# An attention stage reordered: maxima through four banks, rope, norm and statistics in the first part of each body, the residual on GpSimd

## The chip, the cores and the metric

The kernel runs on one core of one Trainium2 chip. The metric is the device time of one execution in microseconds (us), start to end. The engines are PE (TensorE, with its weight loads shown apart as PEld), DVE (VectorE), ACT (ScalarE), POOL (GpSimd) and SP (SyncE), which here only issues DMAs.

## The reference

Sixteen batches of 256 rows by 256 columns in float32 go through two gated layers. Layer 0 adds the normalised x times a decayed running sum of `ctx * ctx`, gated, and a feed-forward block whose inputs and hidden values are rounded to a 4-bit grid. Layer 1, which this study is about, is

```python
q = rope(norm(x)); k = rope(ctx); v = ctx            # 16 heads of 16
scores = einsum('bqhd,bkhd->bhqk', q, k) / sqrt(16) + slope[h] * (key - query)
out = einsum('bhqk,bkhd->bqhd', softmax(scores), v)
x = x + tanh(g_xattn[1]) * out
x = x + tanh(g_ffn[1]) * ffn(norm(x))                # block floating point, gelu
```

with the softmax over 256 keys of each row of each head.

## The kernel before

The whole kernel is one program written out by hand: each engine has its own list of instructions, and semaphores tie the lists together. Nothing is planned at run time, so an instruction that waits holds everything behind it on its engine. The program has three stages: layer 0 (to about 340 us of the span), attention (about 340 to 687 us) and the last feed-forward block. x (`xres`) and ctx stay in SBUF for all sixteen batches.

Attention goes batch by batch in a function `at_body(b)` on each engine. Body b works on three batches at a time:

- for batch b, PE computes the transposed scores (`at_scores`, 16 groups u of two 64-row matmuls, two banks `a_ps_s`), ACT takes the exponential (`at_exponent`), PE multiplies by the values (`at_times_v`, 8 groups), ACT copies the product out (`at_pv_out`);
- for batch b+1, PE transposes the stacked q and k (`at_turn`, 8 groups g, two banks `a_ps_t`), ACT copies them (`at_turned`), PE computes the scores once more in the other direction (`at_scores_for_max`, 16 groups m, two banks `a_ps_m`) and DVE takes the maximum of each row (`at_row_max`). PE then transposes the maxima (`at_turn_max`), ACT negates them (`at_max_out`) and SP places them by two DMAs as a row of the stack (`at_place_max`), from where they enter the scores of batch b+1 in the next body;
- for batch b+2, DVE takes the statistics (`at_qk_a`) and normalises (`at_qk_norm`), POOL multiplies by cosines and sines (`at_k_parts`, `at_q_parts`), DVE adds the halves (`at_rope`) and writes the high part (`at_high_part`), and POOL the low part (`at_low_part`): q and k enter the matmuls as two parts to keep float32 precision.

For batch b-1, PE transposes the product back (`at_turn_out`), and DVE divides by the sum of the exponentials, multiplies by the gate and adds to x (`at_add_attention`).

The order of a body on PE is: transposes 0 and 1, output of b-1, transposes 2 to 5, scores 0, transposes 6, scores 1, transposes 7 (here called the first part), then the sixteen maxima groups, each followed by a score group and, after every second score group, a value product (the second part), and at the end the turned maxima of b+1. DVE reduces in the second part, with the rope of q after five groups and its high part after eight. The two tiles `a_ps_t` and `a_ps_m` are two PSUM banks each, the four of scores and products two and two. A maxima group m waits until DVE has reduced group m-2, whose bank it takes. Bodies 14 and 15 also hold the rounding of the last block's weights (`w34_magic` on DVE, `w34_round` on POOL, `turn_w34` on PE). Body 15 has no next batch.

## Time and profile before

| what | value |
|---|---|
| median of 3 runs | 848.79 us (848.14 to 858.55) |
| the profiled execution | 849.06 us, span 847.0 us |
| mean granted clock of PE | 0.952 of full |
| busy: PE, DVE, ACT, POOL | 707.5, 695.7, 488.6, 431.4 us |

The span is from the first to the last instruction of the profiled execution. Busy times are sums over the whole program, whose stages have different limits, so they say little on one of them; the attention stage has to be read by itself, body by body.

### The profile page before, as it was taken

What the parts mean: (1) busy time and instruction counts of PE and PEld (TensorE: products, weight loads), DVE (VectorE), ACT (ScalarE), POOL (GpSimd) and SP (SyncE); (2) the same over time, 40 slices, a digit from 0 to 9 for tenths busy, and PEclk for the clock granted to TensorE, in tenths of its full rate; (3) what the DMA queues carried; (4) which work ended last, traced back from release to release, by engine and by line L of the source; (5) the groups of instructions that cost most, each with busy time, mean ns of one, the idle gap of its engine ahead of it and who ended that gap; (6) DMA issues with size and microseconds to landing.
All of it is one profiled execution on the core that took longest, in us unless ns stands there. A gap on an engine that the chain in (4) does not pass through costs nothing.

```text
span 847.0 us, 16572 instructions
## 1 busy us (share of the span) xinstructions
PE 707.5 (84%) x5075; PEld 514.2 (61%) x5090; DVE 695.7 (82%) x1230; ACT 488.6 (58%) x955; POOL 431.4 (51%) x331
## 2 busy tenths in 40 slices
PE   2365999999999996889999999999999765777775
PEld 1255888888888885556555665656555433444444
DVE  6866888888888878779888889888888658888985
ACT  3343555555554432357777777777777675556553
POOL 3523665556656655444554445554444425655463
PEclk9987999999999999979999999999999897888999
DMA  8710000000000000010000000000001000000011
GB/s 272 221 43 0 1 1 1 0 0 0 0 0 1 1 2 0 1 51 2 2 3 1 1 1 1 1 1 1 1 1 51 2 1 5 34 25 25 26 38 50
DMA packets 17719, 18.35 MB, mean 22 GB/s; under 512 B 1670, under 2 KB 16912, under 8 KB 17680
## 3 DMA queue, kind: packets, MB, share of 16 engines
q1 hardware_dynamic: 17084, 17.66, 6.5%
q8 instruction: 21, 0.34, 0.2%
q10 hardware_dynamic: 596, 0.20, 0.1%
q14 instruction: 18, 0.15, 0.1%
HBM read 13.39 MB, written 4.19 MB: 21 GB/s over the span
## 4 chain that ended last, share of the span: by engine, by line
PE 51%; DVE 22%; issue 12%; ACT 7%; POOL 5%; DMA 1%; DVEq 1%; POOLq 0%; ACTq 0%; SPq 0%
PE ps_o L528 9%; PE a_ps_t L567 7%; PE a_ps_m L585 6%; DVE maxima L1509 5%; PE a_ps_pv L621 4%; DVE f_ps_small L1594 4%; PE ps_gu L492 4%; PE ps_gu L494 4%; PE ps_gu L493 4%; PE a_ps_s L606 3%; DVE f_hcode L1610 2%; PE a_ps_pv L629 1%; ACT stack_t L920 1%; PE f_ps_h L709 1%; ACT probs L929 1%
## 5 line engine op out<-in xcount | busy, mean ns | idle before, releaser
L1509 DVE TENSOR_REDUCE maxima<-a_ps_m 128x2 f32<-128x512 f32 x256 | 166.1, 685 | 36.5 <-PE a_ps_m L585 35.7
L929 ACT ACTIVATE probs<-a_ps_s 128x512 f32<-128x512 f32 x256 | 149.4, 602 | 43.5 <-PE a_ps_s L606 41.1
L585 PE MATMUL a_ps_m<-stack_t 64*128 64x256 f32 x512 | 109.1, 332 | 19.7 <-DVE maxima L1509 16.7
L585 PEld LDWEIGHTS a_ps_m<-stack_t 64*128 64x128 f32 x512 | 69.5, 192 | 79.3 <-DVE maxima L1509 49.9
L606 PE MATMUL a_ps_s<-stack_t 64*128 64x256 f32 x512 | 100.5, 310 | 4.6 <-ACT probs L929 3.7
L1152 POOL TENSOR_TENSOR stack<-roped,stack 128x512 f32<-128x512 f32 x32 | 42.7, 1335 | 116.2 <-DVE stack L1499 114.7
L528 PE MATMUL ps_o<-w2t,hqt 128*128 128x256 f32 (+1 forms) x384 | 99.6, 394 | 1.2 <-ACT hqt L857 0.7
L492 PE MATMUL ps_gu<-w1h,yth 128*128 128x352 f32 x256 | 86.8, 339 | 4.7 <-DVE h L1322 4.7
L621 PE MATMUL a_ps_pv<-probs,v_aug 128*32 128x256 f32 x1024 | 83.5, 398 | 2.9 <-ACT probs L929 2.7
L920 ACT CAST stack_t<-a_ps_t 128x512 fp32r<-128x512 f32 x128 | 71.0, 588 | 23.5 <-PE a_ps_t L567 22.2
L567 PE MATMUL a_ps_t<-idf,stack 128*128 128x128 f32 x512 | 76.0, 289 | 8.7 <-POOL stack L1152 4.3
L494 PE MATMUL ps_gu<-w1h,ytl 128*128 128x352 f32 x256 | 83.3, 325 | 0.0
L493 PE MATMUL ps_gu<-w1l,yth 128*128 128x352 f32 x256 | 83.3, 325 | 0.0
L528 PEld LDWEIGHTS ps_o<-w2t,hqt 128*128 128x128 f32 (+1 forms) x384 | 66.7, 190 | 22.1 <-issue 12.4
L606 PEld LDWEIGHTS a_ps_s<-stack_t 64*128 64x128 f32 x512 | 68.9, 188 | 13.5 <-ACT probs L929 7.5
L567 PEld LDWEIGHTS a_ps_t<-idf,stack 128*128 128x128 f32 x512 | 57.6, 146 | 21.9 <-ACT stack_t L920 8.5
L1126 POOL TENSOR_TENSOR hq<-hcode,hscale 128x1408 f32<-128x1408 bf16 x16 | 41.5, 2594 | 56.6 <-DVE hcode L1341 56.6
L849 ACT ACTIVATE sg<-ps_gu 128x352 f32<-128x352 f32 x64 | 29.7, 464 | 67.9 <-PE ps_gu L494 67.9
L1201 POOL TENSOR_TENSOR f_hup<-f_h,f_hmag 128x2048 f32<-128x2048 f32 x16 | 58.2, 3641 | 10.5 <-DVE f_hcode L1610 9.5
L990 ACT ACTIVATE f_h<-f_ps_fc 128x512 f32<-128x512 f32 x64 | 36.1, 596 | 36.2 <-POOL f_hup L1201 36.1
L1322 DVE TENSOR_TENSOR h<-sg,ps_gu 128x352 f32<-128x352 f32 x64 | 33.2, 518 | 28.6 <-ACT sg L849 28.1
L709 PE MATMUL f_ps_h<-idb,f_hcode 128*128 128x128 bf16 x256 | 25.2, 256 | 34.7 <-DVE f_hcode L1610 34.7
(178 smaller groups left out, 1608.9 us busy)
## 6 DMA issues: line engine op xcount, KB each, us to landing
xres<-in_x SPq DMA_DIRECT2D x16, 256.0 KB, 3.2
ctx<-in_ctx SPq DMA_DIRECT2D x16, 256.0 KB, 4.1
out_x<-f_y SPq DMA_DIRECT2D x16, 256.0 KB, 2.1
w1a_raw<-in_w_gate_up SPq DMA_DIRECT2D x1, 1024.0 KB, 5.9
w_raw<-in_w_fc SPq DMA_DIRECT2D x1, 1024.0 KB, 5.4
w_raw<-in_w_proj SPq DMA_DIRECT2D x1, 1024.0 KB, 4.8
w_raw<-in_w_down SPq DMA_DIRECT2D x1, 704.0 KB, 9.9
stack_t<-neg_max_t SPq DMA_DIRECT2D x32, 8.0 KB
```

The costliest lines, as they stand in the source:

```text
L492: nc.tensor.matmul(into, yth[:, kc, c, :], w1h[:, kc, cols], start=kc == 0, stop=False)
L493: nc.tensor.matmul(into, yth[:, kc, c, :], w1l[:, kc, cols], start=False, stop=False)
L494: ins = nc.tensor.matmul(into, ytl[:, kc, c, :], w1h[:, kc, cols], start=False, stop=kc == KD - 1)
L528: ins = nc.tensor.matmul(ps_o[:, c, :], hqt[0:rows, g, n, :], w2t[0:rows, k, :], start=k == 0, stop=k == KH0 - 1)
L567: ins = nc.tensor.transpose(a_ps_t[:, g % 2, (n * C + c) * P:(n * C + c + 1) * P], a_stack[:, b.par, which, c, 2 * pair:2 * pair + 2, :].r ...
L585: ins = nc.tensor.matmul(a_ps_m[:, half, n, :], a_stack_t[b.par][rows, 0, pair, c * P:(c + 1) * P], a_stack_t[b.par][rows, 1, pair, :], st ...
L606: ins = nc.tensor.matmul(a_ps_s[:, half, n, :], a_stack_t[b.par][rows, 1, pair, kc * P:(kc + 1) * P], a_stack_t[b.par][rows, 0, pair, :], ...
L621: ins = nc.tensor.matmul(a_ps_pv[32 * n:32 * n + 32, quad % 2, 0:T], a_v_aug[:, b.par, kc, 4 * quad + n, :], a_probs[:, (2 * g + n % 2) % ...
L920: nc.scalar.copy(a_stack_t[b.par][:, g % 2, pair:pair + 2, :].rearrange("p a t -> p (a t)"), a_ps_t[:, g % 2, :]).then_inc(a_t, 1)
L929: nc.scalar.activation(a_probs[:, u % 8], a_ps_s[:, u % 2], ACT.Exp).then_inc(a_exp, 1)
L1201: nc.gpsimd.tensor_tensor(f_blocks(f_hup[:, :]), f_blocks(f_h[:, b.par]), f_spread(f_hmag[:, b.par], F_NBH), ALU.add).then_inc(f_g_hup, 1)
L1509: nc.vector.tensor_reduce(a_maxima[:, b.par, c, 4 * quad + half:4 * quad + half + 3:2], a_ps_m[:, half], X, ALU.max).then_inc(a_v_max, 1)
```

## The change

Five things are done together.

1. Maxima groups use four banks: of the pairs of groups 0 to 7, pairs 2, 4 and 6 (groups 4, 5, 8, 9, 12, 13) go to the transposes' banks `a_ps_t`, the others to `a_ps_m`. Group m then waits for group m-4 (from m = 6 on), groups 4 and 5 wait for ACT's copies of transposes 6 and 7, and transposes 0 and 1 of the next body wait for the reductions of groups 12 and 13.
2. The turned maxima of batch b+1 move from the end of body b to the next body, after its transposes 0 and 1; on ACT their copy moves behind the copy of transpose 0.
3. DVE's part of a body is reordered: rope and high part of k for b+2, division for b-1, rope and high part of q for b+2, statistics for b+4, norm for b+3, all ahead of the reductions, among which nothing is left. Ahead of body 0 DVE does the statistics of batches 1 to 3 and the norm of 1 and 2 (rope and high part of batch 1 among the reductions). The queue of POOL follows: low parts of b+2, q parts of b+3, residual, rstd of b+4, k parts of b+3.
4. The residual add goes from DVE to POOL (`at_add`), and the gate into ACT's copy of ctx into the values (`at_v_of`), a copy that becomes a multiplication.
5. The two semaphores that counted all steps of q and k are split by step, and the loops of POOL and DVE leave four batches at the end written out, not two. The last block's statistics wait for the residual.

The diff, without the renamed semaphores of the functions `at_qk_a`, `at_qk_norm`, `at_rope` and `at_high_part`; these also wait that their buffer of the batch before is read (`a_qn` by POOL's q parts, `a_roped` by the low parts):

```diff
@@ -286,6 +288,17 @@
         f_ps_o = psum("f_ps_o", [P, C, D])
         keep.enter_context(banks)
 
+        def max_bank(m):
+
+
+            pair, half = m // 2, m % 2
+            if pair >= 2 and pair % 2 == 0:
+                return a_ps_t[:, half, :].rearrange("p (a t) -> p a t", t=T)
+            return a_ps_m[:, half]
+
+        def group_in_same_max_bank(m):
+            return m - 4 if m >= 6 else m - 2
+
         f_ps_x = f_ps_h0[:, 0:KD * C * P // 2]
         f_mv = f_small[:, 0:4 * C].rearrange("p (a c s) -> p a c s", a=2, c=C)
...
@@ -555,11 +565,11 @@
             def at_turn(b, g):
 
                 if g == 0:
-                    pe.wait_ge(a_g_qk, upto(g_qk_steps(b), b, "q_lo"))
+                    pe.wait_ge(a_g_low, upto(G_LOW, b, "q_lo"))
                 if g >= 2:
                     pe.wait_ge(a_t, b.count(TG, g - 1))
                 elif b.shifted(-1):
-                    pe.wait_ge(a_t, b.shifted(-1).count(TG, TG + g - 1))
+                    pe.wait_ge(a_v_max, b.shifted(-1).count(MU, 2 * LAST_IN_TURN_BANKS + g + 1))
                 which = g % 2
...
@@ -576,13 +586,15 @@
                 pe.wait_ge(a_t, b.count(TG, 2 * quad + 2))
                 if m == 0 and b.shifted(-1):
                     pe.wait_ge(a_mt, b.shifted(-1).count(1, 1))
-                if m >= 2:
-                    pe.wait_ge(a_v_max, b.count(MU, m - 1))
+                if m in (4, 5):
+                    pe.wait_ge(a_t, b.count(TG, TG + m - 5))
+                elif m >= 2:
+                    pe.wait_ge(a_v_max, b.count(MU, group_in_same_max_bank(m) + 1))
                 elif b.shifted(-1):
                     pe.wait_ge(a_v_max, b.shifted(-1).count(MU, MU + m - 1))
                 for n in range(2):
                     pair = 2 * quad + n
-                    ins = nc.tensor.matmul(a_ps_m[:, half, n, :], a_stack_t[b.par][rows, 0, pair, c * P:(c + 1) * P],
+                    ins = nc.tensor.matmul(max_bank(m)[:, n, :], a_stack_t[b.par][rows, 0, pair, c * P:(c + 1) * P],
                                            a_stack_t[b.par][rows, 1, pair, :], start=True, stop=True)
                 ins.then_inc(a_t_m, 1)
...
@@ -633,6 +645,7 @@
             def at_body(b):
                 nxt = b.shifted(1)
                 if not nxt:
+                    at_turn_max(b)
                     pe.wait_ge(a_mt, B)
                     turn_w34(0)
                     turn_w34(1)
@@ -641,6 +654,8 @@
                         at_turn_out(b.shifted(-1))
                     if nxt:
                         at_turn(nxt, g)
+                        if g == 1:
+                            at_turn_max(b)
                 u = 0
                 for g in range(6, TG):
                     at_scores(b, u)
@@ -666,8 +681,6 @@
                     ff_fc(lead[0], 0)
                     ff_fc(lead[0], 1)
                 at_times_v(b, PG - 1)
-                if nxt:
-                    at_turn_max(nxt)
 
             def ff_turn_input(b):
...
@@ -909,8 +921,8 @@
                     act.wait_ge(a_t_pv, b.shifted(-2).count(PG, PG))
                 elif b.i == 0:
                     act.wait_ge(a_v_aug_laid, 1)
-                nc.scalar.copy(a_v_aug[:, b.par, :, :, 0:HD].rearrange("p c h d -> p (c h) d"),
-                               tiles(ctx, b).rearrange("p c (h d) -> p (c h) d", d=HD)).then_inc(a_v, 1)
+                nc.scalar.mul(a_v_aug[:, b.par, :, :, 0:HD].rearrange("p c h d -> p (c h) d"),
+                              tiles(ctx, b).rearrange("p c (h d) -> p (c h) d", d=HD), gates[:, 1:2]).then_inc(a_v, 1)
...
@@ -943,9 +955,12 @@
             def at_body(b):
                 nxt = b.shifted(1)
                 if nxt:
-                    for g in range(6):
+                    at_turned(nxt, 0)
+                    at_max_out(b)
+                    for g in range(1, 6):
                         at_turned(nxt, g)
                 else:
+                    at_max_out(b)
                     w34_out(0)
                     w34_out(1)
                 for u in range(2):
@@ -966,8 +981,6 @@
                     if not nxt and u == 14:
                         ff_input_out(lead[0])
                 at_pv_out(b, 3)
-                if nxt:
-                    at_max_out(nxt)
 
             def ff_norm(b):
                 act.wait_ge(f_v_shift, b.count(1, 1))
@@ -1045,7 +1058,6 @@
                 at_turned(first, g)
             for g in range(4):
                 l0_hidden_out(last, g)
-            at_max_out(first)
             over_batches(act, at_body)
 
             for u in range(4):
...
+                nc.gpsimd.tensor_tensor(a_part_sin[:, 0, :], qb, a_sin[:, :], ALU.mult).then_inc(a_g_q, 1)
+
+            def at_add(b):
+                pool.wait_ge(a_v_out, upto(V_OUT, b, "share1"))
+                nc.gpsimd.tensor_tensor(tiles(xres, b), tiles(xres, b), a_attn[:, :, :], ALU.add).then_inc(a_g_add, 1)
 
             def at_body(b):
-                nxt2 = b.shifted(2)
+                nxt2, nxt3, nxt4 = b.shifted(2), b.shifted(3), b.shifted(4)
                 if nxt2:
-                    at_k_parts(nxt2)
-                    at_rstd(nxt2)
                     at_low_part(nxt2, 1)
-                    at_q_parts(nxt2)
                     at_low_part(nxt2, 0)
-                elif b.shifted(1):
+                if nxt3:
+                    at_q_parts(nxt3)
+                if b.shifted(-1):
+                    at_add(b.shifted(-1))
+                if nxt4:
+                    at_rstd(nxt4)
+                if nxt3:
+                    at_k_parts(nxt3)
+                if b.shifted(1) and not nxt2:
                     w34_round(0)
                     w34_round(1)
 
@@ -1236,18 +1261,23 @@
             at_low_part(first, 1)
             at_low_part(first, 0)
             l0_hidden_quantised(last)
+            at_rstd(second)
             at_k_parts(second)
-            at_rstd(second)
+            at_q_parts(second)
             at_low_part(second, 1)
-            at_q_parts(second)
             at_low_part(second, 0)
-            over_batches(pool, at_body)
+            at_rstd(third)
+            at_k_parts(third)
+            at_q_parts(third)
+            at_rstd(fourth)
+            over_batches(pool, at_body, ATT_AHEAD)
 
             for b in lead[:3]:
                 ff_input_rstd(b)
             ff_input_up(lead[0])
             ff_input_rstd(lead[3])
             ff_input_up(lead[1])
+            at_add(last)
             ff_input_rstd(lead[4])
             ff_input_up(lead[2])
             ff_input_rstd(lead[5])
...
                     bank = a_ps_pv[:, c, :].rearrange("p (h s) -> p h s", s=2 * HD)
                     dve.wait_ge(a_v_out, upto(V_OUT, b, f"recip{c}"))
                     nc.vector.tensor_tensor(a_attn[:, c, :].rearrange("p (h d) -> p h d", d=HD), bank[:, :, 0:HD],
                                             a_denom[:, c, :].unsqueeze(2).to_broadcast([P, NH, HD]), ALU.mult).then_inc(a_v_out, 1)
-                dve.wait_ge(a_v_out, upto(V_OUT, b, "share1"))
-                nc.vector.scalar_tensor_tensor(tiles(xres, b).rearrange("p c d -> p (c d)"), a_attn[:, :, :].rearrange("p c d -> p (c d)"),
-                                               gates[:, 1:2], tiles(xres, b).rearrange("p c d -> p (c d)"),
-                                               ALU.mult, ALU.add).then_inc(a_v_out, 1)
 
             def at_body(b):
-                nxt2 = b.shifted(2)
+                nxt2, nxt3, nxt4 = b.shifted(2), b.shifted(3), b.shifted(4)
                 if nxt2:
-                    at_qk_a(nxt2)
                     at_rope(nxt2, 1)
                     at_high_part(nxt2, 1)
-                    at_qk_norm(nxt2)
-                if b.shifted(-1):
-                    at_add_attention(b.shifted(-1))
+                if b.shifted(-1):
+                    at_share(b.shifted(-1))
+                if nxt2:
+                    at_rope(nxt2, 0)
+                    at_high_part(nxt2, 0)
+                if nxt4:
+                    at_qk_a(nxt4)
+                if nxt3:
+                    at_qk_norm(nxt3)
                 if b.shifted(1) and not nxt2:
                     w34_magic(0)
                 for m in range(MU):
@@ -1540,13 +1575,11 @@
                         at_row_max(b.shifted(1), m)
                     if m == 7 and b.shifted(1) and not nxt2:
                         w34_magic(1)
-                    if nxt2 and m == 5:
-                        at_rope(nxt2, 0)
-                    if nxt2 and m == 8:
-                        at_high_part(nxt2, 0)
 
             def ff_input_stats(b):
                 p = b.par
+                dve.wait_ge(a_g_add, b.count(1, 1))
+                dve.sem_inc(f_alone, 1)
                 for c in range(C):
                     nc.vector.bn_stats(f_stats[:, p, c, :], tiles(xres, b)[:, c, :]).then_inc(f_v_ln, 1)
                 if b.shifted(-2):
...
@@ -1674,19 +1707,25 @@
             l0_add_ffn(last.shifted(-1))
             at_lay(1)
             at_qk_a(second)
-            at_rope(second, 1)
-            at_high_part(second, 1)
             at_qk_norm(second)
             for m in range(MU):
                 at_row_max(first, m)
+                if m == 3:
+                    at_rope(second, 1)
+                    at_high_part(second, 1)
                 if m == 5:
                     l0_add_ffn(last)
                     at_rope(second, 0)
-                if m == 8:
                     at_high_part(second, 0)
-            over_batches(dve, at_body)
-
-            dve.wait_ge(a_g_qk, len(G_QK) * B)
+                if m == 9:
+                    at_qk_a(third)
+                if m == 12:
+                    at_qk_norm(third)
+                if m == 14:
+                    at_qk_a(fourth)
+            over_batches(dve, at_body, ATT_AHEAD)
...
@@ -1701,7 +1740,7 @@
             ff_input_stats(lead[3])
             ff_input_codes(lead[1])
             ff_input_shift(lead[3])
-            at_add_attention(last)
+            at_share(last)
             ff_input_magic(lead[2])
```

## Rows read from the trace of the kernel before

**Rows 1.** Timeline of ACT, copies of the negated maxima: start us, us, what.

```profile
366.95 0.37 ACT L941 ACTIVATE neg_max_t<-a_ps_m 16x256 fp32r<-16x256 f32 x1 [13.60 <-PE a_ps_m L592]
...
387.84 0.37 ACT L941 ACTIVATE neg_max_t<-a_ps_m 16x256 fp32r<-16x256 f32 x1
...
642.53 0.37 ACT L941 ACTIVATE neg_max_t<-a_ps_m 16x256 fp32r<-16x256 f32 x1
...
665.59 0.37 ACT L941 ACTIVATE neg_max_t<-a_ps_m 16x256 fp32r<-16x256 f32 x1
```

**Rows 2.** Busy us over two bodies: window, length, PE PEld DVE ACT POOL, clock.

```profile
426.39:465.49 39.10, 36.22 (x344) 23.42 (x340) 34.56 (x67) 30.09 (x60) 18.83 (x14) 1.00 0.01 2
```

**Rows 3.** Waits in that window: us in total, times, longest us.

```profile
PEld a_ps_m L585 <- DVE maxima L1509: 8.2, 17, 0.9
```

**Rows 4.** Timeline of PE in the body of batch 5.

```profile
465.49 0.39 PE L592 MATMUL a_ps_m<-idf,maxima 128*16 128x128 f32 x2
465.71 1.07 PE L567 MATMUL a_ps_t<-idf,stack 128*128 128x128 f32 x8
466.62 1.04 PE L629 MATMUL a_ps_pv<-idf,pv_t 128*128 128x128 f32 x8
...
469.84 0.50 PE L606 MATMUL a_ps_s<-stack_t 64*128 64x256 f32 x2
...
471.87 0.52 PE L585 MATMUL a_ps_m<-stack_t 64*128 64x256 f32 x4
...
472.55 0.64 PE L621 MATMUL a_ps_pv<-probs,v_aug 128*32 128x256 f32 x8
...
474.50 0.64 PE L621 MATMUL a_ps_pv<-probs,v_aug 128*32 128x256 f32 x8
...
475.78 0.64 PE L621 MATMUL a_ps_pv<-probs,v_aug 128*32 128x256 f32 x8
...
484.23 0.64 PE L621 MATMUL a_ps_pv<-probs,v_aug 128*32 128x256 f32 x8 [0.21 <-ACT probs L929]
```

**Rows 5.** Timeline of the same body, rows of DVE and POOL.

```profile
465.35 0.74 DVE L1463 BATCH_NORM_STATS2 a_stats<-xres 128x6 f32 x2
...
466.55 0.69 DVE L1487 TENSOR_TENSOR roped<-part_cos,part_sin 128x512 f32<-128x512 f32 x1
...
467.37 0.69 DVE L1499 CAST stack<-roped 128x1024 fp32r<-128x1024 f32 x1
...
468.14 1.29 POOL L1152 TENSOR_TENSOR stack<-roped,stack 128x512 f32<-128x512 f32 x1
468.34 1.56 DVE L1478 TENSOR_SCALAR qn<-xres,a_mv,a_rstd 128x256 f32 x2
...
471.03 0.78 DVE L1523 SCALAR_TENSOR_TENSOR xres<-attn,gates,xres 128x512 f32 x1 [0.17 <-DVE attn L1520]
...
472.49 2.57 DVE L1509 TENSOR_REDUCE maxima<-a_ps_m 128x2 f32<-128x512 f32 x4 [0.68 <-PE a_ps_m L585]
...
476.82 0.68 DVE L1487 TENSOR_TENSOR roped<-part_cos,part_sin 128x512 f32<-128x512 f32 x1
```

**Rows 6.** Chain that ended last, in the body of batch 15.

```profile
666.68 1.91 DMA stack_t<-neg_max_t
```

**Rows 7.** Page, costliest groups, ACT exponentials: busy us, mean ns, idle before.

```profile
L929 ACT ACTIVATE probs<-a_ps_s 128x512 f32<-128x512 f32 x256 | 149.4, 602 | 43.5 <-PE a_ps_s L606 41.1
```

**Rows 8.** Source line of the norm: duration ns min, median, max.

```profile
L1478 DVE TENSOR_SCALAR qn<-xres,a_mv,a_rstd x32: 400/409/1387, 325.0 to 626.7; 128x256 f32 x24, 128x256 f32<-128x256 f32 x8
```

**Rows 9.** Timeline of DVE in the bodies of batches 0 and 14.

```profile
373.95 1.39 DVE L1509 TENSOR_REDUCE maxima<-a_ps_m 128x2 f32<-128x512 f32 x2 [3.33 <-PE a_ps_m L585]
...
654.79 2.27 DVE L1443 TENSOR_REDUCE w_magic<-w_raw 128x64 f32<-128x2048 f32 x1
```

**Rows 10.** Busy us by engine, granted clock is the last but two.

```profile
501.00:503.00 2.00, 2.00 (x18) 1.01 (x18) 1.29 (x2) 1.09 (x2) 2.00 (x3) 0.55 0.00 0
```

**Rows 11.** Timeline of PE in that window.

```profile
501.94 1.03 PE L621 MATMUL a_ps_pv<-probs,v_aug 128*32 128x256 f32 x8
```

79 lines of the change are left out of this document (44 added, 35 removed).

## The prediction

> **What bounds the kernel now.** I first read the clock and the span, then the page's busy shares, then the attention stage, the only stage the change touches in any quantity. The rows of the copy that takes out a batch's negated maxima come once per body [rows 1]: from 387.84 to 642.53 us thirteen bodies pass (those of batches 1 to 13), 254.69 / 13 = 19.59 us each. Body 0 took 387.84 - 366.95 = 20.89, body 14 took 665.59 - 642.53 = 23.06. Then the busy time of each engine over two whole bodies [rows 2]: of 39.10 us PE has 36.22, DVE 34.56, ACT 30.09, POOL 18.83. No engine is full, so waits must be named, and in that stretch the longest that belongs to the queue order is PE's weight load for a maxima group waiting on DVE's row maxima, 17 times [rows 3].
>
> One body on PE [rows 4] has two parts. First part: the turned maxima at 465.49, transposes for the next batch from 465.71, the turned output at 466.62, scores from 469.84, and the first maxima group at 471.87; that is 6.4 us. Second part: sixteen maxima groups between scores and value products, 471.87 to the last product's end at about 484.8, 12.9 us. There PE stands still for DVE, up to 0.9 us at a time [rows 3], and the eight value products (L621), which come 1.28 us apart where nothing stalls (474.50 to 475.78), take 484.23 - 472.55 = 11.68 us for seven intervals, not 7 x 1.28 = 8.96. DVE in the same body [rows 5]: its first part is full from 465.35 to 471.81, then it reduces, four in 2.57 us (0.64 each), and inside this it must also do the rope and the high part of q (0.68 each, the row at 476.82 and a like one for the cast). With two banks a reduction's end, a wait, a matmul and a start lie in series; one late PE item and both stand. So the second part is set by the two-bank exchange between PE and DVE, and DVE's extra 1.3 us in it.
>
> **The change, part by part, per body.** I take time 0 as the start of the turned maxima on PE.
>
> (a) *Turned maxima after the first two transposes.* The two transposes need only the maxima of groups 12 and 13, which DVE has behind it, so 0.91 us of PE work (465.71 to 466.62) now stands where PE waited for the last reductions. In return the chain from maxima to the bias row in the scores gets shorter cover. The negated maxima are out 0.43 + 0.37 = 0.80 after time 0; the row needs 668.59 - 665.96 = 2.63 us more [rows 1, 6], so it is there at 3.43. PE: 0.22 for the turned maxima, then 469.84 - 466.62 = 3.22 for turned output and four transposes, so it asks at 3.44. The cover was 0.9 us and is now nothing: each 0.1 us of slower landing costs 0.1 us per body. I take 3.45. The first maxima group follows 471.87 - 469.84 = 2.03 later, at 5.48, the first value product 0.68 later (472.55), at 6.16.
>
> (b) *Four banks, rope and cast of q out of the second part.* PE's seven intervals are at best 8.96 us. Worst: the banks help nothing and only the two DVE steps (1.3) go: 11.68 - 1.3 = 10.4. Between them ACT decides: an exponential is 0.6 us [rows 7] against two per interval, and the scores keep two banks, so whatever ACT puts between two exponentials (three copies of products and the copy of v, some 0.25 and 0.55 beside their neighbours, together 1.3) holds PE's next score. I let 0.9 of it through, since PE's order gives back part: 9.9. With the last product (0.57) and the two transposes (0.91), the body is 6.16 + 9.9 + 0.57 + 0.91 = 17.5 us. Both ends give 16.6 and 18.0.
>
> (c) *Is DVE then the bound?* First part, from [rows 5]: rope and cast of k 0.82 + 0.76, share 1.13 (469.90 to 471.03), rope and cast of q 1.58, statistics 1.20 (465.35 to 466.55), scaled rstd 0.2 and norm. The norm is two instructions, 1.56 us in this body, but the median of one is 409 ns and the longest 1387 [rows 8]: in each pair one is held while POOL's low part (468.14, 1.29) runs. In the new order POOL's low part of q starts when the cast of q ends and is over about when the norm begins, so I take 0.8 for the pair (1.56 if it still collides). Sum 6.5 to 7.2, and 16 x 0.64 = 10.2: 16.7 to 17.4, just under PE's 17.5. The trace shows the collision. The Trainium skill, SBUF — State Buffer, section Who interferes with whom, says that casts and tensor_scalar in two-port mode and GpSimd exclude each other, whoever issues first; by that rule alone each such pair that still meets would put DVE at 17.4 and the body at no more than my 17.5, so it moves nothing but the range.
>
> (d) *Residual on GpSimd.* DVE loses 0.78 us and a 0.17 wait (471.03). POOL gets one two-input instruction of the low part's size, 1.29 us, or up to 1.75 beside DVE. POOL's body becomes 9.4 + 1.3 to 1.8, about 11 of 17.5; queued behind the add are the rstd of batch b+4 and the k parts of b+3, both needed a body later: covered, by some 2 us for the k parts. If that cover were gone, the rope of k, first on DVE, would wait. DVE's add took 0.78 and POOL's sort of instruction 1.29. The Trainium skill, GPSIMD Engine Reference, section Engine selection, says that elementwise adds belong on VectorE, GpSimd being about twice as slow; here that speaks against the step only if POOL were the late engine. The gate moves into ACT's copy of v (0.61 now): nothing, at most 0.05.
>
> (e) *Ahead of body 0.* DVE gets statistics of batches 2 and 3 and the norm of batch 2, 1.2 + 1.2 + 1.0 (1.7 if held) = 3.4 to 4.1 us, and loses the moved rope and cast from before its first reduction (1.5) and the gaps of the two banks, some 1.4. Body 0 starts 1 to 2 us later. But there DVE sat idle 3.33 us before its first reduction at 373.95 [rows 9], which takes this. Its second part then gains like the others, 1.8. I take 2 us of gain (bounds -1 and +4). What bodies 12 and 13 lose of DVE work is the same 3.4 and off PE's path.
>
> (f) *Body 14.* Its 23.06 hold two weight magnitudes of 2.3 + 0.4 on DVE, one among the reductions (654.79) [rows 9]. DVE: start at 5.9, 16 reductions 10.2, magnitude 2.7: 18.8, plus 1.2 for a low clock that remains: 20.0, a gain of 3 (bounds 0 and 5). POOL's two rounding steps start after the add, 1.3 us, which is covered by its wait for the second magnitude.
>
> (g) *Feed-forward start.* DVE loses one add before the first statistics, 0.7; the statistics now wait for POOL's add of a batch long done. 0.5. The last add waits on POOL between two things of batches 1 and 4, at most 1 us either way.
>
> Sum: 13 x (19.59 - 17.5) = 27.2, plus 2 + 3 + 0.5 = 32.7. The profiled execution is 849.06 us (span 847.0), so 816.4; it stands 0.27 above the median of 848.79, so 816.1. I predict 816.
>
> **Rivals.**
> 1. *PE at its own pace.* ACT's pieces hide wholly and DVE is free of collisions: body 16.7, 13 x 0.8 = 10 less: 806, and 801 with the best of (e) and (f). For: PE's 1.28 intervals occur back to back. Against: two banks of scores.
> 2. *The four banks buy nothing.* Scores on two banks, or the groups 4 and 5 waiting for the turned copies of transposes 6 and 7, hold PE so that it never runs ahead: 10.4 in (b), body 18.1, 849 - 13 x 1.5 - 2 = 827; with nothing from (e) or (f), 830. This is also the case where the change does only part of what it says. For: ACT is at 30.09 of 39.10 already.
> 3. *A new wait eats it all.* The landing of the bias row, now without cover, or POOL's k parts late: it takes 1.2 us a body more than in rival 2 to leave under 2% of gain. 833 to 866.
> 4. *Slower: the clock.* The granted clock fell to 0.55 for some 4 us about 501 to 503 [rows 10] in a body of 20.58. The low level there is 1.2 GHz. A value product takes PE 1.03 us there against 0.64 [rows 4, 11], and the groups between lengthen alike or more: PE's work is 1.7 times as long, so each us at the low level costs 0.4 us once PE is the bound. If the denser body kept PE at it, it would need (33 + 17) / 0.4 = 125 us, half the stage, to end above 866. Against: thirteen bodies show one such fall, and PE idles less after the change, not more. The Trainium skill, TensorE: Matmul & The Clock Gate, section A second HAM failure mode, describes a clock that swings when matmul groups cycle through PSUM banks with short idles; by it this case would have more of these falls.
>
> **How the numbers follow.** Forecast (808 to 824): 0.52. Rival 1 (800 to 808): 0.15. Rival 2 (824 to 832): 0.22. Rival 3: 0.08. Rival 4: 0.03. Range 801 to 830: from the bottom of rival 1 to the top of rival 2. About 2% (17 us) is what can be told from no change: below 832 lie 0.90, within 0.07, above 866 0.03.
>
> **What would show it.** In the profile after: maxima copies 17.5 us apart in the loop; value products about 1.4 apart on average; DVE's first part 6.5 us with norm instructions of 0.41; DVE's wait by PE's maxima groups small and PE's wait for maxima nearly gone, with PE waiting for exponentials in its place; scores at 3.45 after the turned maxima with a DMA named as releaser. Wrong would be: the first reduction waiting on PE by over 0.5 us, rope of k waiting for POOL, or more stretches at the low clock.

## The result, and the profile after

The changed kernel takes 836.84 us (median of 4 runs, 834.57 to 839.60) beside 849.38 us of the kernel before on the same chip: a ratio of 0.984, with an interval of 0.980 to 0.987: a gain clear of noise, but under 2%. It is 12.5 us where 33 were forecast; the time lies above the range of 801 to 830. The profiled execution took 837.79 us (span 836.0, clock 0.920), 11.27 less than the one of before.

The same landmark as in [rows 1], the copies of the negated maxima in the timeline of ACT, kernel after:

```profile
370.00 0.37 ACT L953 ACTIVATE neg_max_t<-a_ps_m 16x256 fp32r<-16x256 f32 x1 [3.81 <-PE a_ps_m L604]
...
389.52 0.37 ACT L953 ACTIVATE neg_max_t<-a_ps_m 16x256 fp32r<-16x256 f32 x1
...
629.99 0.37 ACT L953 ACTIVATE neg_max_t<-a_ps_m 16x256 fp32r<-16x256 f32 x1
...
650.97 0.37 ACT L953 ACTIVATE neg_max_t<-a_ps_m 16x256 fp32r<-16x256 f32 x1
```

They cut the 11.0 us by which the spans differ into four pieces. The copy now comes after the first two transposes of the next body, 0.92 us later in the order of work; that shift is taken out of the first and the third piece (body 15 has no transposes ahead of it).

| piece | before | after | gain | forecast |
|---|---|---|---|---|
| to the end of body 0 (second copy) | 387.84 | 389.52 | -0.8 (raw -1.7) | 2 |
| bodies 1 to 13 | 13 x 19.59 | 13 x 18.50 | 14.2 | 27.2 |
| body 14 | 23.06 | 20.98 | 1.2 (raw 2.1) | 3 |
| from the last copy to the end | 181.4 | 185.0 | -3.6 | 0.5 |

So the loop gives half of what was expected, and every other piece falls short too. About 1 us of the 14.2 is not the change's: in the kernel before the body of batch 6 took 20.58 us at a granted clock of 0.92, the other twelve 19.51 on average, while after the change bodies 1 to 13 all show 1.00. Busy us over two bodies of after, the view of [rows 2]:

```profile
481.90:518.90 37.00, 36.00 (x342) 24.00 (x340) 32.23 (x65) 29.95 (x61) 18.92 (x16) 1.00 0.00 1
```

PE's busy time is what it was, 36.00 against 36.22, and only the length around it has shrunk. The waits in that stretch (us in total, times, longest) are no longer the seventeen of [rows 3]. "PEld" rows are waits of a weight load, part of which passes while matmuls still run:

```profile
ACT probs L941 <- PE a_ps_s L618: 3.3, 9, 0.7
...
PEld a_ps_m L597 <- DVE maxima L1541: 3.5, 8, 0.5
...
PEld a_ps_t L597 <- DVE maxima L1541: 1.6, 4, 0.4
...
DVE maxima L1541 <- PE a_ps_m L597: 1.3, 4, 0.4
```

PE's timeline of one body, which answers to [rows 4]:

```profile
518.90 0.38 PE L604 MATMUL a_ps_m<-idf,maxima 128*16 128x128 f32 x2
...
522.51 0.50 PE L618 MATMUL a_ps_s<-stack_t 64*128 64x256 f32 x2
...
524.53 0.51 PE L597 MATMUL a_ps_m<-stack_t 64*128 64x256 f32 x4
...
525.22 0.64 PE L633 MATMUL a_ps_pv<-probs,v_aug 128*32 128x256 f32 x8
525.91 0.50 PE L597 MATMUL a_ps_m<-stack_t 64*128 64x256 f32 x2
...
527.17 0.64 PE L633 MATMUL a_ps_pv<-probs,v_aug 128*32 128x256 f32 x8
...
528.42 0.64 PE L633 MATMUL a_ps_pv<-probs,v_aug 128*32 128x256 f32 x8
...
530.44 0.64 PE L633 MATMUL a_ps_pv<-probs,v_aug 128*32 128x256 f32 x8
...
532.03 0.64 PE L633 MATMUL a_ps_pv<-probs,v_aug 128*32 128x256 f32 x8
...
535.99 0.64 PE L633 MATMUL a_ps_pv<-probs,v_aug 128*32 128x256 f32 x8
```

Scores are asked for at 3.61 after the turned maxima, the first maxima group comes at 5.63, the first value product at 6.32 (forecast 3.45, 5.48, 6.16). The seven intervals between the eight value products take 535.99 - 525.22 = 10.77 us, where 9.9 were forecast. Two of them carry most: 525.22 to 527.17 (1.95) and 528.42 to 530.44 (2.02). The same body on DVE and POOL, beside [rows 5]:

```profile
524.11 0.73 DVE L1509 TENSOR_SCALAR qn<-xres,a_mv,a_rstd 128x256 f32 x2 [0.18 <-DVE a_rstd L1504]
525.16 2.57 DVE L1541 TENSOR_REDUCE maxima<-a_ps_m 128x2 f32<-128x512 f32 x4 [0.32 <-PE a_ps_m L597]
...
527.47 1.28 POOL L1190 TENSOR_TENSOR xres<-xres,attn 128x512 f32 x1
...
528.28 1.29 DVE L1541 TENSOR_REDUCE maxima<-a_ps_t 128x2 f32<-128x512 f32 x2 [0.54 <-PE a_ps_t L597]
```

The norm's pair costs 0.73, free of collision, and the residual 1.28 on a POOL that is 18.92 of 37.00 us busy. The first interval shows why it did not shorten: groups 0 to 3 all go to `a_ps_m`, two banks, so group 2 (525.91) starts when the reduction of group 0 (525.16 to about 525.8) is over. For groups 2 and 3 the four banks do not exist.

### The profile page after: what moved, and what is told of

Same layout as the page of the kernel before. It is cut to its first block, busy times and chain, and to the rows that moved or that the text cites. A ratio compares the mean times of both kernels' runs of the same rounds, so it can differ in the third digit from the quotient of the medians.

```text
span 836.0 us, 16572 instructions
## 1 busy us (share of the span) xinstructions
PE 713.6 (85%) x5090; PEld 522.9 (63%) x5090; DVE 681.1 (81%) x1214; ACT 487.4 (58%) x955; POOL 434.5 (52%) x347
## 4 chain that ended last, share of the span: by engine, by line
PE 59%; DVE 16%; issue 9%; ACT 7%; POOL 4%; DMA 3%; SPq 1%; DVEq 0%; POOLq 0%; ACTq 0%
PE ps_o L538 9%; PE a_ps_t L577 7%; PE a_ps_pv L633 7%; PE a_ps_s L618 5%; PE a_ps_m L597 5%; PE ps_gu L502 4%; PE ps_gu L504 4%; PE ps_gu L503 4%; DVE f_ps_small L1627 4%; PE a_ps_t L597 3%; DMA ctx<-in_ctx 3%; DVE f_hcode L1643 2%; DVE maxima L1541 2%; PE a_ps_pv L641 1%; PE f_ps_h L722 1%
## 5 line engine op out<-in xcount | busy, mean ns | idle before, releaser
L941 ACT ACTIVATE probs<-a_ps_s 128x512 f32<-128x512 f32 x256 | 147.6, 601 | 29.6 <-PE a_ps_s L618 27.4
L1541 DVE TENSOR_REDUCE maxima<-a_ps_m 128x2 f32<-128x512 f32 x160 | 105.5, 685 | 17.8 <-PE a_ps_m L597 16.9
L577 PE MATMUL a_ps_t<-idf,stack 128*128 128x128 f32 x512 | 78.1, 294 | 9.3 <-POOL stack L1164 4.7
L1541 DVE TENSOR_REDUCE maxima<-a_ps_t 128x2 f32<-128x512 f32 x96 | 64.2, 685 | 12.2 <-PE a_ps_t L597 9.6
L597 PE MATMUL a_ps_m<-stack_t 64*128 64x256 f32 x320 | 66.7, 325 | 4.2 <-DVE maxima L1541 3.4
L597 PEld LDWEIGHTS a_ps_m<-stack_t 64*128 64x128 f32 x320 | 43.7, 189 | 34.9 <-DVE maxima L1541 21.1
```

Source lines behind the costliest of these rows:

```text
L577: ins = nc.tensor.transpose(a_ps_t[:, g % 2, (n * C + c) * P:(n * C + c + 1) * P], a_stack[:, b.par, which, c, 2 * pair:2 * pair + 2, :].r ...
L597: ins = nc.tensor.matmul(max_bank(m)[:, n, :], a_stack_t[b.par][rows, 0, pair, c * P:(c + 1) * P], a_stack_t[b.par][rows, 1, pair, :], sta ...
L941: nc.scalar.activation(a_probs[:, u % 8], a_ps_s[:, u % 2], ACT.Exp).then_inc(a_exp, 1)
L1541: nc.vector.tensor_reduce(a_maxima[:, b.par, c, 4 * quad + half:4 * quad + half + 3:2], max_bank(m), X, ALU.max).then_inc(a_v_max, 1)
```

## The experiments

The seven intervals are written from left to right, the mean of nine bodies (3 to 11) of each profile; "body" is the mean of bodies 1 to 13; "copy 0, 1" are the first two of the copies above. In the kernel before, in "before, four banks" and in "turned maxima late" the copies stand 0.92 us earlier in the order of work than in the others. A sum is that of the rounded intervals, good to 0.02. The medians come from several groups of runs, each with the kernel before beside it (its median 849.4 to 851.3), so wholes are compared by the ratio; "changed, again" shares its group with "the same, turned maxima early", the short magnitude and the combination. In the mean of before, body 6 with its low clock is included; without it the intervals are 1.96 1.28 2.83 1.29 1.80 1.28 1.28, together 11.71.

| kernel | median us | ratio to before, interval | body | the seven intervals | sum | copy 0, 1 |
|---|---|---|---|---|---|---|
| before | 849.38 | | 19.59 | 1.96 1.28 2.83 1.30 1.84 1.32 1.29 | 11.82 | 366.95, 387.84 |
| changed | 836.84 | 0.984, 0.980 to 0.987 | 18.50 | 1.96 1.25 1.98 1.59 1.41 1.34 1.22 | 10.75 | 370.00, 389.52 |
| changed, again | 837.46 | 0.983, 0.980 to 0.985 | 18.49 | as above | 10.73 | 370.04, 389.99 |
| two banks | 843.55 | 0.990, 0.988 to 0.992 | 18.91 | 1.96 1.28 2.33 1.28 1.71 1.24 1.32 | 11.12 | 370.18, 390.55 |
| before, four banks | 836.49 | 0.982, 0.979 to 0.985 | 18.81 | 1.95 1.25 1.97 1.50 1.50 1.27 1.30 | 10.74 | 364.79, 385.57 |
| the same, turned maxima early | 830.29 | 0.976, 0.974 to 0.979 | 18.48 | 1.96 1.25 1.97 1.50 1.49 1.28 1.29 | 10.74 | 365.57, 385.05 |
| changed, turned maxima late | 836.82 | 0.985, 0.982 to 0.988 | 18.57 | as changed | 10.73 | 369.37, 389.19 |
| changed, add on VectorE | 836.45 | 0.984, 0.981 to 0.987 | 18.80 | first 2.34 | 11.12 | 369.26, 389.03 |
| other order of banks | 833.23 | 0.977, 0.975 to 0.980 | 18.26 | 1.69 1.30 1.92 1.64 1.36 1.39 1.17 | 10.47 | 368.72, 390.84 |
| copy of v late | 835.33 | 0.981, 0.979 to 0.984 | 18.52 | 1.96 1.24 1.98 1.25 1.74 1.24 1.32 | 10.73 | 369.83, 389.75 |
| half exponentials | 822.87 | 0.969, 0.965 to 0.972 | 17.59 | 1.96 1.25 1.55 1.58 1.25 1.24 1.00 | 9.83 | 370.25, 390.19 |
| half maxima | 829.00 | 0.977, 0.973 to 0.981 | 18.26 | as other order of banks | 10.47 | 367.96, 387.91 |
| half of both | 809.05 | 0.952, 0.949 to 0.955 | 17.06 | 1.42 1.25 1.55 1.58 1.25 1.24 1.00 | 9.29 | 368.20, 388.15 |
| half of both, copy of v late | 805.49 | 0.946, 0.943 to 0.950 | 16.79 | 1.42 1.25 1.55 1.24 1.32 1.24 1.00 | 9.02 | 368.26, 388.19 |
| half exponentials, other order | 818.23 | 0.961, 0.957 to 0.965 | 17.41 | 1.31 1.29 1.53 2.00 1.24 1.25 1.00 | 9.62 | 368.74, 388.75 |
| short magnitude | 833.82 | 0.980, 0.978 to 0.982 | 18.50 | as changed | 10.74 | 369.86, 389.80 |
| combination | 834.41 | 0.981, 0.979 to 0.984 | 18.77 | 1.70 1.29 1.93 2.09 1.44 1.49 1.07 | 11.01 | 364.41, 384.04 |
| the same, order of banks alone | 833.56 | 0.981, 0.978 to 0.983 | 18.77 | 1.69 1.30 1.93 2.10 1.44 1.49 1.07 | 11.02 | 364.32, 384.54 |
| start light | 834.22 | 0.982, 0.978 to 0.985 | 18.51 | as changed | 10.74 | 366.85, 388.97 |

**What the four banks are worth.** They are taken out of the changed kernel, and put alone into the kernel before.

```diff
 def max_bank(m):
     pair, half = m // 2, m % 2
-    if pair >= 2 and pair % 2 == 0:
-        return a_ps_t[:, half, :].rearrange("p (a t) -> p a t", t=T)
     return a_ps_m[:, half]
...
 def group_in_same_max_bank(m):
-    return m - 4 if m >= 6 else m - 2
+    return m - 2
...
```

> The changed kernel with the maxima groups back on two banks, all else kept. Theory A (after the change PE sets the body by its own work and by the exponentials, and the four banks only let it run ahead of DVE): the seven value-product intervals grow from 10.77 us towards 11.4, the body from 18.50 to about 19.1, the whole by 8 us to about 845. Rival B (the four banks do nothing, since groups 2 and 3 still wait for the reductions of groups 0 and 1 and nothing after them waits for DVE; the gain came from DVE's moved steps): body 18.5 to 18.6, the whole within 2 us of 837.

> The kernel before with the four banks alone: the order of DVE, POOL and ACT as before, turned maxima at the end of the body, where PE's first two transposes of the next body now wait for the reductions of groups 12 and 13. Theory A (four banks cover the rope and the cast that stood among the reductions): the interval around value product 3, 2.81 us before, falls to about 2.1, the body from 19.59 to about 18.7, the whole by 12 us to about 837, as much as the whole change gives. Rival B (four banks give little by themselves): body 19.3 or more, the whole above 844.

The two answers differ: in the changed kernel the banks give 18.91 - 18.49 = 0.42 us a body, in the kernel before 19.59 - 18.81 = 0.78 (0.70 without the low clock of body 6), and by themselves they reach the whole time of the complete change (ratios of 0.982 and 0.983, whose intervals overlap). The seven intervals are the same 10.74. What the reorder of DVE was to give in the second part, the banks had given already. The kernel with two banks also shows that reorder by itself: 11.12 against 11.71, so taking the rope and the cast of q from among the reductions gave 0.6 us and not their whole 1.3.

**The other parts, one by one.** The turned maxima go back to the end of the body, or come early in the version with the banks alone (the same edit the other way round):

```diff
-                        if g == 1:
-                            at_turn_max(b)
...
                 at_times_v(b, PG - 1)
+                if nxt:
+                    at_turn_max(nxt)
...
```

> The changed kernel with the turned maxima back at the end of the body (and ACT's copy of them behind its last copy of products), all else kept. Theory A (each of the parts gains in its own place): PE stands again for the last reductions, body from 18.50 to 18.8, the whole by 4 us to about 841. Rival B (with the maxima group ahead by four banks the last reductions are done in time and the step gives nothing): body 18.5, the whole within 1 us of 837.5.

> The kernel before with the four banks and the turned maxima moved behind the first two transposes, and nothing else: DVE and POOL keep their old order, the residual stays on DVE. Theory A (DVE's new order buys almost nothing in the loop once four banks cover it, and costs some 3 us ahead of body 0): first negated maxima at about 366, bodies 18.5 to 18.7, the whole 834 to 836, at least as fast as the whole change. Rival B (the moved rope, norm and statistics are needed for the pace): bodies 18.9 or more, the whole above 839.

With the old order of DVE the early place gives 0.33 us a body (18.81 to 18.48), with the new one 0.08. The traces show why. From the start of the last value product to that of the turned maxima at the end of a body (bodies 3 to 11) the kernel before takes 0.57 us, which is the product alone: PE did not stand there at all. With four banks PE gets there sooner, and with rope and cast still among the reductions DVE is late, 0.86; with the new order it is 0.63. The early place takes away these 0.29 and 0.06. The version with banks and turned maxima alone, 830.29 us, is the fastest of all that compute the reference, 7 us under the changed kernel in the same group of runs.

The residual is put back on VectorE:

```diff
-                if b.shifted(-1):
-                    at_add(b.shifted(-1))
...
+                dve.wait_ge(a_v_out, upto(V_OUT, b, "share1"))
+                nc.vector.tensor_tensor(tiles(xres, b), tiles(xres, b), a_attn[:, :, :], ALU.add).then_inc(a_v_out, 1)
...
```

> The changed kernel with the residual add back on DVE (0.7 to 0.8 us in its first part; the gate stays in ACT's copy of v). Theory A (DVE is not what the first part waits for now: PE's first maxima group and not DVE's queue releases the first reduction, which stood 0.3 to 0.4 us before it): of the 0.7 us only 0.35 come through, body 18.7 to 18.9, the whole by 3 to 5 us. Rival B (covered, since the exchange over groups 0 to 3 has slack): body 18.5, the whole within 1 us of 837.5.

Body 18.80, 0.31 more: the add (0.69 and a wait of 0.20) pushes the first reduction back, and the first interval goes to 2.34. The whole is nevertheless the same within its interval; the profile had the first two copies 0.5 to 1.0 earlier than the two profiles of the changed kernel, and a shorter last part (183.0 for 185.0 and 187.8). Beside the 18.48 of the version with the old order and the add on VectorE, this says that the new order alone loses 0.3 a body, and the move to GpSimd gives it back.

**What fills 10.75 us.** First the order of the banks (m t m t m m t m, with `a_ps_t` for pairs 1, 3 and 6), so that groups 2 and 3 need not wait for the reductions of 0 and 1; then ACT's copy of v behind the exponentials.

```diff
-            if pair >= 2 and pair % 2 == 0:
+            if pair in (1, 3, 6):
...
-            return m - 4 if m >= 6 else m - 2
+            return 2 * (0, 0, 0, 1, 2, 4, 3, 5)[m // 2] + m % 2
...
```

> The changed kernel with the pairs of maxima groups on the banks m t m t m m t m (before: m m t m t m t m, m the maxima's own two banks, t the transposes'), so that groups 2 and 3 no longer wait for the reductions of groups 0 and 1. Theory A (the missed 0.87 us of the second part is mostly that first exchange, an interval of 1.95 us between the first two value products in the traces of both kernels): that interval falls to 1.3 to 1.5, the body from 18.50 to about 18.0, the whole by 6 to 8 us to about 830. Rival B (the scores' two banks and the exponentials set the pace, so what PE gains early it waits for later): the interval falls but the seven together stay at 10.6 or more and the whole at 835 to 838.

```diff
-                    if u == 8 and nxt:
-                        at_v_of(nxt)
...
+                if nxt:
+                    at_v_of(nxt)
                 at_pv_out(b, 3)
```

> The changed kernel with ACT's gated copy of v moved from between exponentials 8 and 9 to behind exponential 15, where ACT stands 0.76 us before its last copy of products. Theory A (exponentials and what ACT puts between them hold PE's scores in the middle of the second part): the interval of value products 3 and 4 falls from 1.6 to 1.3, the body from 18.50 to 18.1 to 18.2, the whole by 4 to 5 us. Rival B (PE's own work is the bound there, the copy is hidden): body 18.45 to 18.55, the whole within 1 us of 837.

The first interval moved by 0.27 only, not by the half microsecond expected: once the reductions no longer hold it, the rest goes with the exponentials (1.31 in a kernel below that shortens them under the same order of banks). The late copy took 0.34 from one interval (1.59 to 1.25) and gave 0.33 to the next: it shifts a wait, the sum stays. In the changed kernel the copy stands among exponentials like this (timeline of ACT):

```profile
529.34 1.12 ACT L941 ACTIVATE probs<-a_ps_s 128x512 f32<-128x512 f32 x2
530.35 0.71 ACT L924 ACTIVATE v_aug<-ctx,gates 128x512 f32 x1
530.97 1.22 ACT L941 ACTIVATE probs<-a_ps_s 128x512 f32<-128x512 f32 x2
532.08 0.37 ACT L947 COPY pv_t<-a_ps_pv 128x256 f32<-128x256 f32 x1
```

Then each engine's main instruction is made shorter, one at a time and both together. These kernels leave out part of the work: from batch 1 on the exponentials are taken for half of the queries only, or the maxima over half of the keys. Their output is not the reference's, and they serve only to show who waits for whom; PE's work is unchanged.

```diff
+                n = slice(0, T // 2 if b.shifted(-1) else T)
-                nc.scalar.activation(a_probs[:, u % 8], a_ps_s[:, u % 2], ACT.Exp).then_inc(a_exp, 1)
+                nc.scalar.activation(a_probs[:, u % 8, :, n], a_ps_s[:, u % 2, :, n], ACT.Exp).then_inc(a_exp, 1)
```

```diff
-                nc.vector.tensor_reduce(a_maxima[...], max_bank(m), X,
+                nc.vector.tensor_reduce(a_maxima[...], max_bank(m)[:, :, T // 2:T], X,
...
```

> The changed kernel in which ACT takes the exponential of only the first 128 of 256 queries of each head from batch 1 on (the rest keeps old values, so that output is wrong by that), 16 exponentials a body at about 0.35 instead of 0.60 us, no other engine changed. Theory A (exponentials and PE's own work together pace the second part): the seven intervals fall from 10.75 to 10.2 or less, the body by 0.5 or more. Rival B (ACT hides; PE's matmuls and DVE's reductions alone set it): intervals 10.6 or more, body above 18.3.

> The changed kernel in which DVE reduces only the later 128 of 256 keys of each row (a maximum too low in part of the rows, no other work changed), 16 reductions a body at about 0.42 instead of 0.68 us. Theory A (DVE still holds PE at the first exchange, groups 2 and 3, and a little later): first interval from 1.96 to about 1.5, the seven from 10.75 to 10.1, body 17.8 to 17.9. Rival B (PE and ACT alone set the second part): intervals 10.6 or more, the body 18.3 or more. Whichever engine's halving gives more is what the second part waits for.

> The changed kernel with the exponentials of the scores over half of each row's columns (the rest of the weights is left as it was in the buffer) and the maxima's reductions over half of their columns, so that the output is not the reference's. It asks what is left of the seven intervals once both ScalarE and VectorE are quick. Alone, half exponentials gave 9.83 us for the seven and half maxima 10.47. Theory A (TensorE's own work is the floor and the two savings add): 9.83 - 0.28 = 9.55 us, body 17.585 - 0.24 = 17.35 us, whole 818 to 822. Theory B (with short exponentials the reductions no longer hold anything): intervals 9.8, body 17.6, whole as with half exponentials alone, 823. Theory C (my forecast's term of 9.9 was TensorE's floor plus little, and the floor is really lower): intervals under 9.2, body under 17.1.

What the two instructions cost then, groups of ACT and DVE over 400 to 600 us, of the one and of the other kernel:

```profile
L942 ACT ACTIVATE probs<-a_ps_s 128x256 f32<-128x256 f32 x185 | 69.1, 386 | 41.1 <-PE a_ps_s L618 37.9
```

```profile
L1541 DVE TENSOR_REDUCE maxima<-a_ps_m 128x2 f32<-128x256 f32 x110 | 43.5, 420 | 32.0 <-PE a_ps_m L597 32.0
```

An exponential of 386 ns for 600 takes 0.92 us from the seven intervals; a reduction of 420 ns for 686 only 0.28, the same as the other order of banks gave. Together they take 1.46, more than the sum of 1.20. The difference lies in the first interval: a wait for VectorE lay beside one for ScalarE, 1.96 with both, 1.69 with VectorE's gone, 1.96 with ScalarE's gone, 1.42 with neither. Of the theories on half of both, A (9.55) and C (under 9.2) miss and B (the reductions no longer matter) is refuted; half maxima alone fell between its two theories. DVE now waits for PE before 16 of 32 reductions, over two bodies of the kernel with half of both (us in total, times, longest):

```profile
DVE maxima L1542 <- PE a_ps_m L597: 5.1, 10, 0.8
...
DVE maxima L1542 <- PE a_ps_t L597: 3.2, 6, 0.7
```

One interval still stood out: the fourth, 1.58 us for four groups, with no idle time shown on PE (timeline of PE, then of ACT, in that kernel):

```profile
500.90 0.64 PE L633 MATMUL a_ps_pv<-probs,v_aug 128*32 128x256 f32 x8
...
502.49 0.64 PE L633 MATMUL a_ps_pv<-probs,v_aug 128*32 128x256 f32 x8
```

```profile
501.02 0.71 ACT L924 ACTIVATE v_aug<-ctx,gates 128x512 f32 x1
501.63 0.80 ACT L942 ACTIVATE probs<-a_ps_s 128x256 f32<-128x256 f32 x2
```

The exponentials behind the copy of v end at 502.43, and the product starts 0.06 later. Two more kernels ask whether that copy is the cause, and whether the reductions hold only the first exchange: the half of both with the late copy of v, and half exponentials with the other order of banks (edits as above).

> The kernel with half exponentials and half maxima (its output is not the reference's), and ScalarE's copy of v moved behind the last exponential of the body. The seven intervals were 1.42 1.25 1.55 1.58 1.25 1.24 1.00 = 9.29 with no wait shown in the fourth; it holds four groups like those of 1.25, but the copy of v (0.71 us) stands before its exponentials and ends them at 502.43, 0.06 before the value product at 502.49. Theory A (the fourth interval waits for that copy, and the profile does not name it): fourth interval 1.25, sum 8.96, body 16.7, whole 804 to 806. Theory B (1.58 is TensorE's own): sum 9.29, body 17.06, whole 809.

> The changed kernel with the other order of banks (m t m t m m t m) and half exponentials (its output is not the reference's), all reductions whole. It asks whether what half maxima gave was only the wait of groups 2 and 3 for the reductions of 0 and 1. Theory A (yes): first interval 1.4, sum 9.3, body 17.05, as with half of both. Theory B (short reductions help elsewhere too): first interval 1.69, sum 9.55, body 17.3; whole 812 to 814.

In the first, theory A holds: the fourth interval falls to 1.24, the sum to 9.02, the body to 16.79 and the whole to 805.49 us. In the second, the first interval falls to 1.31 as theory A wanted, but the fourth grows to 2.00, where groups 10 and 11 share banks with 8 and 9; the sum of 9.62 is closer to B's. With quick exponentials and whole reductions the wait for VectorE is moved, not removed. So at most 9.0 of the 10.75 us is TensorE's own. The other 1.7 is waiting: 0.9 goes with the exponentials, about 0.3 with the copy of v once these are short, and the rest, 0.5, with the reductions. The shares hold for this order of taking the waits away: with whole exponentials the copy of v gives nothing and the reductions 0.28.

**Why body 0 starts late.** In the changed kernel some instructions on DVE are held while POOL takes the k parts (timeline of DVE, ahead of body 0):

```profile
345.78 1.23 DVE L1504 TENSOR_SCALAR a_rstd<-a_rstd 128x2 f32<-128x2 f32 x1 [0.81 <-POOL a_rstd L1178]
347.05 1.65 DVE L1509 TENSOR_SCALAR qn<-xres,a_mv,a_rstd 128x256 f32<-128x256 f32 x2
...
364.49 1.64 DVE L1509 TENSOR_SCALAR qn<-xres,a_mv,a_rstd 128x256 f32<-128x256 f32 x2
```

In the loop the same steps take 0.15 and 0.73. This is the exclusion that the Trainium skill states in SBUF — State Buffer, Who interferes with whom, and the trace agrees: 1.1 us more for the first, 0.9 more for each pair. But being held is the smaller part of the delay. The first reduction starts at 348.62 as before (348.72), and the last one ends at 369.31 where it ended at 366.26: what lies between is the statistics of batch 2 (361.14 to 362.33), the rstd and norm of batch 2 (364.12 to 366.05) and the statistics of batch 3 (367.25 to 368.63), 4.5 us among the reductions, about 1 of it held. Then the norm of batch 2 and the statistics of batch 3 are moved behind the last reduction:

```diff
-                if m == 12:
-                    at_qk_norm(third)
-                if m == 14:
-                    at_qk_a(fourth)
...
+            at_qk_norm(third)
+            at_qk_a(fourth)
             over_batches(dve, at_body, ATT_AHEAD)
```

> The changed kernel, but ahead of body 0 alone the norm of batch 2 and the statistics of batch 3 stand behind the last reduction again. Theory A (VectorE's early steps, held up by GpSimd's, are what delays the first body): the first copy of the negated maxima goes from 370.0 back to about 366.7, the second from 389.7 to about 388.5 since body 0 gets the moved steps back in part, whole 1 to 2 us shorter (835.5 to 836.5). Theory B (the later start comes from GpSimd's taking the k parts of rope early): the first copy stays at 369 to 370 and the whole is the same, 837.5.

The stretch ahead of the first copy, busy us of PE, PEld, DVE, ACT, POOL and the clock: first the changed kernel, then start light, then banks and turned maxima alone.

```profile
340.00:370.00 30.00, 23.74 (x112) 17.53 (x111) 25.59 (x51) 7.14 (x16) 17.13 (x14) 0.73 0.00 1
```

```profile
340.00:366.85 26.85, 22.47 (x112) 16.74 (x111) 22.58 (x45) 7.13 (x16) 13.94 (x11) 0.82 0.00 1
...
366.85:388.97 22.12, 19.13 (x164) 11.79 (x163) 19.15 (x35) 16.22 (x32) 12.28 (x10) 0.92 0.17 50
```

```profile
340.00:365.57 25.57, 21.87 (x109) 16.14 (x108) 19.71 (x40) 7.05 (x16) 13.22 (x10) 0.83 0.00 1
```

The clock is not what moves the first copy: the second profile of the changed kernel has 0.78 in that stretch and the same 370.04. In start light the first copy is at 366.85, as theory A had it, but body 0 then takes 22.12 us, and the second copy has gained only 0.6 to 1.0. The whole (834.22, from 831.34 to 837.97) can't be told from the changed kernel's: ratios of 0.982 and 0.983 with intervals that overlap, and copy 14 stands at 629.64 against 629.99 and 630.39, under 1 us earlier. So the early steps do cause the late first copy, yet moving them cures little: the change runs statistics and norm a batch further ahead. Up to the second copy DVE is busy 25.59 + 16.41 = 42.0 us in the changed kernel (16.41 in the same view from 370.00 to 389.52), 22.58 + 19.15 = 41.7 in start light, and 19.71 + 15.43 = 35.1 with the old lead. That work has to be paid before the loop is full.

**Body 14.** The second weight's magnitude is taken over 4 of each 32 elements, so that its scales come out too small; no other work changes:

```diff
-                nc.vector.tensor_reduce(to, f_blocks((w3_raw, w4_raw)[n][:, :]), X, ALU.max,
+                nc.vector.tensor_reduce(to, f_blocks((w3_raw, w4_raw)[n][:, :])[:, :, 0:(QB1, 4)[n]], X, ALU.max,
```

> The changed kernel in which the second weight magnitude, which stands among the reductions of body 14, looks at 4 of each 32 elements (about 0.5 instead of 2.3 us; w_proj's scales are then too small, no other work changed). Theory A (PE stands for that magnitude, and the clock falls behind the stall and stays low into body 15): body 14 falls from 21.0 to 18.8 to 19.2, the stretch from the last negated maxima to the first gelu from 24.8 to 22.4 to 23.0, the whole by 3 to 5 us. Rival B (the low clock comes from elsewhere): body 14 falls by the 1.8 us of the reduction, the stretch behind it stays at 24 or more.

Body 14 takes 18.09 instead of 20.98 (19.72 in the second profile of the changed kernel), so the magnitude is worth 1.6 to 2.9 there. The place in the changed kernel, PE's timeline, and the windows behind it, their last but two number the clock:

```profile
645.17 0.35 PE L597 MATMUL a_ps_t<-stack_t 64*128 64x256 f32 x1 [1.19 <-DVE maxima L1541]
```

```profile
645.00:650.00 5.00, 4.83 (x38) 2.32 (x38) 4.17 (x8) 1.96 (x4) 4.92 (x2) 0.58 0.00 0
650.00:655.00 5.00, 4.54 (x32) 3.38 (x28) 0.39 (x2) 2.67 (x4) 1.86 (x1) 0.50 0.01 3
```

PE stands 1.19 us and then works ten microseconds at 0.50 to 0.58, the level of 1.2 GHz. That the wait is what brings the low clock is not shown: the second profile of the changed kernel (below) has the same wait of 1.19 us, at 645.60, and the clock stays at 1.00 from 645 to 650 and 0.97 from 650 to 655. Without the magnitude the clock is full there too, and falls to 0.50 at 655 to 660. Where the fall comes differs between executions of one kernel. From the last copy to the first gelu the short magnitude takes 23.86 us, between what its two theories wanted. Its whole is 833.82 us, a ratio of 0.980 whose interval overlaps that of the changed kernel.

**The second profile, and the combination.** The changed kernel itself ran once more, to see how much of the last part repeats.

> The changed kernel once more, on the chip of the next three. Theory A (the layer order, not chance, makes its start and its end longer): first negated maxima at 369 to 370 us, bodies 18.50, from the last negated maxima to the first gelu 24 us or more against 22.4 in the kernel before. Rival B (the end is a matter of the clock granted in one execution): that last stretch differs from 24.8 by over 1 us.

Its loop repeats within 0.01 us a body. From the last copy to the first gelu it took 27.67 us where the first profile had 24.78 and the kernel before 22.41; over all the kernels that stretch lay between 21.1 and 27.7. It goes with the granted clock of the stretch (the last number but two), here for the changed kernel, the same again, before, and the changed kernel with the other order of banks:

```profile
650.97:675.75 24.78, 21.87 (x156) 12.67 (x157) 9.88 (x38) 18.47 (x33) 6.96 (x8) 0.76 0.01 2
```

```profile
650.11:677.78 27.67, 22.10 (x156) 11.81 (x157) 9.89 (x38) 18.48 (x33) 8.26 (x8) 0.69 0.01 2
```

```profile
665.59:688.00 22.41, 16.73 (x155) 9.75 (x157) 10.51 (x39) 18.37 (x33) 4.85 (x6) 1.00 0.01 3
```

```profile
649.77:672.31 22.54, 16.96 (x156) 9.76 (x157) 9.90 (x38) 18.25 (x33) 6.15 (x8) 1.00 0.01 3
```

The version with the late copy of v has a clock of 1.00 there too and takes 22.59. So at full clock the stretch is within 0.2 us of the kernel before, with the whole change in place, and 2.4 of the -3.6 in the last piece go with a lower clock, which differs from one execution to the next. The other 1.2 lie behind the first gelu, a stretch of 159.0 us before and 157.3 to 160.8 in the other kernels.

Then the two things that had looked good were added to the fastest version, and after that only one of them.

> The last kernel with the bank order m t m t m m t m and ACT's copy of v behind exponential 15 as well. Theory A (first exchange gone, late copy harmless, short start kept): bodies 18.2 to 18.4, the whole 829 to 832, under the changed kernel by 5 us or more. Rival B (DVE's rope and cast of q among the reductions now take the slack that the order gains): bodies 18.6, the whole 835 or more.

> The kernel before with four banks and the turned maxima's early place, plus the other order of banks (m t m t m m t m), nothing else. Its parent took 830.3 us with a body of 18.48 and intervals of 10.74; with this order and the later copy of v together it took 834.4, body 18.77, intervals 11.01. Theory A (the order of banks is at fault: with the rope of q between VectorE's reductions, groups 2 and 3 come free later in the other bank): body about 18.75, intervals 11.0, whole 834. Theory B (the later copy of v was at fault, and the order of banks helps here as in the changed kernel, by 0.23 a body): body 18.2 to 18.3, intervals 10.5, whole 827.

Both cost 0.29 a body, the order of banks alone as much as the two: it is at fault, the copy of v is neutral. Timeline of DVE in the version with the order alone:

```profile
470.12 1.28 DVE L1522 TENSOR_REDUCE maxima<-a_ps_t 128x2 f32<-128x512 f32 x2
471.31 0.68 DVE L1522 TENSOR_REDUCE maxima<-a_ps_m 128x2 f32<-128x512 f32 x1
471.91 0.69 DVE L1512 CAST stack<-roped 128x1024 fp32r<-128x1024 f32 x1
472.51 1.97 DVE L1522 TENSOR_REDUCE maxima<-a_ps_m 128x2 f32<-128x512 f32 x3
```

In this order pairs 4 and 5 stand in the same banks, in the old order of DVE the rope of q stands behind six reductions and the cast behind nine, and so the cast comes between the reductions of groups 8 and 9, for which groups 10 and 11 wait: the fourth interval is 2.10 for 1.50. In the changed kernel nothing stands there, and the same order gains 0.23. The tables of who shares a bank and who is queued between two reductions have to be made together.

## Why the prediction was wrong

The direction and the main mechanism held: the change is faster, the exchange between PE and DVE held up the second part, and ACT's exponentials came next. The size did not: 11.3 us in the profile for 32.7.

- **(b), the step that failed.** The seven intervals "I let 0.9 of it through ...: 9.9" measured 10.77 in the body read and 10.75 on average: 0.87 x 13 = 11.3 of the 21.4 us missing. The term that was mis-sized is the waits of the two banks, which I let go wholly. Groups 0 to 3 stay in two banks by the diff itself, so the first interval stayed at 1.96 (0.28 with the other order of banks), and once the exponentials are short the reductions still cost 0.5. The best case of 8.96 has company in the 9.02 of the last kernel, but that is not made of seven equal intervals of 1.28: it runs from 1.00 to 1.55. The 0.9 for ScalarE is near the 0.92 of the half exponentials by luck. I had put it down to the copies between exponentials; moving the copy of v alone gave nothing, and what gave 0.92 was the exponentials' own length. With the copy of v on top ACT's share is 1.2.
- My worst case for (b), 10.4, was too low as well. It took away DVE's two steps in full (1.3); the kernel with two banks, which comes closest to that case, has 11.12 where the kernel before has 11.71, so they give 0.6. With four banks they give nothing: 10.74 with the steps among the reductions and without. Part of it is a reading: the 8.2 us of [rows 3] are waits of weight loads, while PE's own matmuls waited for the maxima 1.4 us in the same stretch.

```profile
PE a_ps_m L585 <- DVE maxima L1509: 1.4, 2, 0.7
```

- **(a)** 3.61, 5.63, 6.32 for 3.45, 5.48, 6.16: each 0.16 late, 2 us over thirteen bodies. Besides, the turned maxima were moved out of a place where the kernel before did not wait: from the last value product of a body to the first of the next it took 7.84 us, and takes 7.76.
- **(c)** DVE's first part, 517.80 to 524.84 = 7.0 us for 6.5 to 7.2, and the norm (0.73 for 0.8) were right. DVE's first reduction waits 0.32 for PE, so DVE was not late there.
- **(d)** The add takes 1.28 on POOL, covered, as forecast. Its worth on DVE, 0.31 a body, was measured in the new order only.
- **(e)** Forecast +2, measured -0.8. The added steps took 4.5 us for my 3.4 to 4.1. The rope and cast taken from ahead of the first reduction, 1.5, saved nothing, since the scaled rstd there waited 0.81 for POOL and was then held 1.1: the reduction begins at 348.62 for 348.72. Of the 3.33 us of idle 0.73 are left. The bound of -1 contains the result.
- **(f)** 1.2 for 3 (in the second profile 23.06 - 19.72 - 0.92 = 2.4, at a clock of 1.00 where the first has 0.88).
- **(g)** The 0.5 can't be told apart under a clock that varies. What I had left out is that the stretch behind the last copy varies by several microseconds between profiles.

Rival 2 gave 827 to 830 and was the nearest in time, with its reason in part: TensorE is held through the whole second part, though by exponentials and by the groups still in two banks, not by the turned copies of transposes 6 and 7 (group 4 starts at 527.74, over two microseconds after them). It still lay short, since it too stood on 10.4. Rival 1 (806, body 16.7) is TensorE at its own pace, and that is near what the kernel shows whose exponentials, reductions and copy of v are out of the way: 805.49, 16.79. It takes half of both engines' work away to get there. The time lies in the range given to rival 3, without its mechanism: no rope of k waits for POOL, and PE waits for the bias row seven times in thirteen bodies, 1.7 us in all by its weight loads, 0.7 at most, in the body of batch 3, where two copies lie 18.98 us apart and in the second profile 18.96 (18.5 elsewhere). Its price was also wrong as written: 1.2 us a body more is what leads from the forecast to 832; from rival 2 it takes 0.15 to 0.4. Rival 4 did not come in the loop, where the granted clock of bodies 1 to 13 is 1.00 in both profiles.

## What to carry to other kernels

Before a term is written for more buffers, list for each use which earlier use has its buffer, and what is queued before that release: four banks helped only the groups that really alternated, and a good order of banks under one queue was a bad one under another. A term for the engine behind the one freed is split into its instructions, since waits that lie beside each other do not go one by one. When several parts of a change aim at the same wait, price each as the only one and then the rest on top: here two of five gave everything, and the rest, with its lead by one more batch, put the second copy 4 to 5 us later (389.52 and 389.99 for 385.05) for nothing in the loop. Last, a second profile of the same kernel is worth its cost before a difference in one stretch is explained.

## What was not expected of the hardware

A `tensor_scalar` of 128x2 elements, 0.15 us by itself, took 1.23 while GpSimd worked at its k parts: it ended at 347.01, GpSimd's instruction at 346.98. PE's rows can hide a wait: an interval of 1.58 us with no idle time shown fell to 1.24 when the copy ahead of its exponentials went. The granted clock in the last bodies differs between two profiles of the same kernel: after the last copy the first gelu came 24.78 us later in one, 27.67 in the other, and the same wait of 1.19 us was followed by 0.50 in one and by 1.00 in the other.
